# A decoder layer on one core: the Mamba work of four batches as one pipeline instead of two

## The chip, the cores and the metric

The kernel runs on one core of a Trainium2 chip. The metric is the time of one execution on the device in microseconds (us). Before the change three runs took 3520.11, 3522.89 and 3524.64 us; the median, 3522.89 us, is what the prediction is measured against.

## What is computed

One decoder layer, everything in float32, for 4 batches of 1024 tokens with 256 channels each:

```python
out1 = mb(rmsnorm(x, norm1_w))          # a Mamba block: projection, 4-tap convolution, selective scan, projection
x1   = x + out1
out2 = mb(rmsnorm(x1, norm2_w))         # the same Mamba weights a second time
out2 = memory_attend(out2, proj_write_w, proj_read_w, decay)
x = layernorm(x + (x1 + out2))
x = layernorm(x + cross_attention(x, context))      # 16 heads over 64 context tokens
x = layernorm(x + mixture_of_experts(x))            # best 2 of 8 experts
```

The heart of the Mamba block is a recurrence over the tokens, for 512 channels and 16 states:

```python
h = h * exp(d_t * A) + (d_t * u_t) * B_t
y = sum over states of h * C_t
```

The second Mamba pass of a batch needs the first pass's result (x1), and the second half of a batch's tokens needs the state h that the first half ended with. Batches don't depend on each other before the experts.

## The kernel before, in words

**Items, chunks and slots.** A batch's 1024 tokens are two halves of 512. One *item* is one half of one batch in one of the two passes: with u the batch within a pair, m the pass and h the half, the eight items of a pair come in the order u, then h, then m (`item_at`). An item has 64 *chunks*: one state and one block of 128 channels each. A chunk is one scan instruction of 128x512 on VectorE (`scan`, L1614), which takes its factors from ScalarE (`decay`, L931), its other input from a PSUM bank that TensorE fills by transposes (`fill`, L1181), and whose result GpSimd multiplies by a row of C (`weigh_c`, L720) and TensorE adds up (`add_y`, L1200). The time in which the 64 scans of one item run is called a *slot* below.

**The order is written out by hand.** Every engine runs the same loop `for c in range(-2 * CHUNKS, RUN + TAIL)`, and `when(c)` says which items are at which stage at chunk c: item s is scanned; item p = s + 1 goes through its input stage (normalise, project, convolve, make the step sizes); item p2 = s + 2 has its squares summed; item k = s - 1 leaves (gate, output projection). A table of numbers (`IN`, `SILU`, `SLOPE`, `TURN`, `MO` and so on) says at which of the 64 chunks each piece stands. So in the middle of the pipeline the scans of one item, the input stage of the next and the output stage of the one before share each slot. Two slots' worth of loop ahead of the first scan hold only input stages, and a tail of up to 64 chunks after the last scan holds only an output stage.

**Two groups.** `for g0 in range(GROUPS)` runs this pipeline twice, for batches 0 and 1 and for batches 2 and 3, eight items each. After each pipeline come the memory and the cross attention of that pair's two batches, one after the other (the *body* of a batch). `o2_dram` holds the second pass's result of the pair until its batch's body loads it. The buffers of the bodies and those of the pipeline lie in the same SBUF arena; only `xin` (x, later x1, of the two batches) keeps its place through both. After the second group come the experts.

**Names and lines used below.** VectorE: `convolve` (L1562), `sum_halo` (L1446 to L1455: what the second half needs of the first half's last three tokens), `times_u` (L1603), the multiply by the gate (L1535), the additions of `leave` (L1545 in pass 0, L1550 in pass 1), the normalisation that ends a body (L1521), the memset that begins one (L1652). GpSimd: `add_bias` (L672, one instruction of 128x1024 at the start of each pass-0 item's slot) and `normalise` (L685). `normalise` of a group's first item waits until the x2 of the batch before has been stored. SyncE issues the transfers in one queue, in this order: rows of C from `c_dram` (L581, four slots of buffer, one row for four chunks), `keep_o2` (L563), and in the bodies the loads of o2 (L596), x (L599), the next pair's x (L604) and the store of x2 (`keep_x2`, L548).

## Time and profile before

| what | value |
|---|---|
| median of 3 runs | 3522.89 us (3520.11 to 3524.64) |
| the profiled execution, first to last instruction | 3546.8 us |
| TensorE matmul / VectorE / ScalarE / GpSimd busy | 79% / 67% / 54% / 50% |
| first pipeline, first scan to last scan | 89.24 to 1067.75 us |
| bodies of batches 0 and 1 | to 1357.09 us |
| second pipeline, first scan to last scan | 1416.99 to 2395.36 us |
| bodies of batches 2 and 3 | to 2681.70 us |
| experts and the end | to 3546.8 us |

Of the profiled execution no other time than its span is on record; it is 23.9 us (0.7%) longer than the median of the runs. The profile's page gives busy shares over the whole span, which mixes stages with different limits. The view of busy time by stretch cuts the span at chosen times; here the cuts are the starts of the slots and the ends of the bodies, which the timeline of VectorE shows.

### The profile page before, as it was taken

How to read it: one execution, taken by the hardware profiler on the slowest of the kernel's cores; microseconds unless marked ns; L12 is line 12 of the kernel's file. 1: busy time of each engine (PE TensorE's matmuls, PEld its weight loads, DVE VectorE, ACT ScalarE, POOL GpSimd, SP SyncE). 2: the span in 40 equal slices, each digit the busy share in tenths (PEclk: the TensorE clock that was granted, in tenths of full speed). 3: DMA queues.
4: the chain of work that ended last, by engine and by line, in shares of the span. 5: the costliest groups of instructions: out<-in, count | busy, mean ns of one | idle time of the engine just before them, and what ended most of it. 6: DMA issues, size and time to landing. Idle time of an engine off the chain costs nothing.

```text
span 3546.8 us, 46325 instructions
## 1 busy us (share of the span) xinstructions
PE 2817.5 (79%) x15402; PEld 2084.2 (59%) x15403; DVE 2358.7 (67%) x3266; ACT 1928.5 (54%) x3239; POOL 1775.1 (50%) x1888
## 2 busy tenths in 40 slices
PE   3888788788887995788788788887996898999910
PEld 1666566666675653666566666675656665766600
DVE  3888988988882444888988988882444332333347
ACT  4877877887781324877887887771331111111100
POOL 1777767777781001777767777781100123222261
PEclk8998999999999896998999999999995799999955
DMA  3110111111111000011111111111102023122131
GB/s 107 31 36 32 34 36 34 34 36 41 40 44 55 28 9 25 31 37 32 35 34 34 34 37 39 40 46 54 36 1 86 33 79 132 49 77 78 50 96 55
DMA packets 101822, 163.32 MB, mean 46 GB/s; under 512 B 16610, under 2 KB 55778, under 8 KB 101634
## 3 DMA queue, kind: packets, MB, share of 16 engines
q1 hardware_dynamic: 80242, 109.94, 9.8%
q0 software_dynamic: 18064, 49.21, 4.1%
q8 instruction: 106, 1.74, 0.2%
q10 hardware_dynamic: 3328, 1.76, 0.2%
q14 instruction: 82, 0.67, 0.1%
HBM read 127.01 MB, written 24.38 MB: 43 GB/s over the span
## 4 chain that ended last, share of the span: by engine, by line
PE 42%; DVE 23%; ACT 13%; issue 11%; DMA 9%; POOL 1%; SPq 0%; another core or an unknown queue 0%; POOLq 0%; DVEq 0%; ACTq 0%
PE psD L1083 14%; DVE arena L1614 9%; PE psD L1181 6%; PE psA L1200 5%; ACT arena L931 4%; DMA write_w_sb<-x_dram,read_w_sb 4%; DMA write_w_sb<-write_w_sb 3%; ACT arena L921 3%; PE psD L1412 3%; DMA read_w_sb<-arena 2%; PE psD L1283 2%; PE psA L1083 2%; PE psA L1258 2%; PE psA L1190 2%; PE psD L1304 2%
## 5 line engine op out<-in xcount | busy, mean ns | idle before, releaser
L720 POOL TENSOR_TENSOR arena<-arena 128x512 f32<-128x512 f32 x1024 | 1154.2, 1154 | 17.8 <-DVE arena L1614 7.4
L1181 PE MATMUL psD<-ident,arena 128*128 128x128 f32 x4096 | 686.7, 293 | 344.4 <-DVE arena L1614 318.3
L1181 PEld LDWEIGHTS psD<-ident,arena 128*128 128x128 f32 x4096 | 482.3, 148 | 605.2 <-DVE arena L1614 375.8
L931 ACT ACTIVATE arena<-arena,negA 128x512 f32<-128x512 f32 x1024 | 719.2, 711 | 26.4 <-DVE arena L1614 25.7
L1614 DVE TENSOR_TENSOR_SCAN arena<-arena,carry,psD 128x512 f32<-128x512 f32 x512 | 641.9, 1269 | 83.3 <-PE psA L1200 75.2
L1614 DVE TENSOR_TENSOR_SCAN arena<-arena,psD 128x512 f32<-128x512 f32 x512 | 612.9, 1208 | 93.4 <-PE psA L1200 75.6
L1200 PE MATMUL psA<-ident,arena 128*128 128x128 f32 x4096 | 645.1, 283 | 0.0
L921 ACT ACTIVATE arena<-arena,bc 128x512 f32<-128x512 f32 x768 | 546.0, 711 | 118.3 <-PE psD L1181 117.6
L1200 PEld LDWEIGHTS psA<-ident,arena 128*128 128x128 f32 x4096 | 510.1, 148 | 2.1 <-issue 2.1
L704 POOL TENSOR_SCALAR arena<-arena,bc 128x512 f32<-128x512 f32 x256 | 180.8, 707 | 460.7 <-PE psD L1181 390.7
L1083 PE MATMUL psD<-arena 128*128 128x512 f32 (+4 forms) x776 | 336.1, 568 | 45.9 <-POOL strip L664 31.1
L1040 ACT ACTIVATE in_w_sb<-in_w_sb 128x512 f32<-128x512 f32 x140 | 88.1, 629 | 468.0 <-DVE in_w_sb L1812 468.0
L1412 PE MATMUL psD<-arena 128*128 128x256 f32 x1120 | 258.4, 384 | 2.9 <-DVE arena L1818 2.9
L823 ACT ACTIVATE arena<-psA 128x512 f32<-128x512 f32 x160 | 91.4, 597 | 300.5 <-PE psA L1258 117.2
L1083 PE MATMUL psD<-arena,in_w_sb 128*128 128x512 f32 x512 | 243.0, 598 | 6.5 <-DVE halo L1573 4.8
L1083 PEld LDWEIGHTS psD<-arena 128*128 128x128 f32 (+1 forms) x776 | 142.5, 194 | 153.0 <-issue 143.3
L1412 PEld LDWEIGHTS psD<-arena 128*128 128x128 f32 x1120 | 210.3, 193 | 31.4 <-DVE arena L1818 4.8
L1812 DVE TENSOR_TENSOR in_w_sb<-psD,arena 128x512 f32<-128x512 f32 x140 | 96.8, 691 | 166.0 <-PE psD L1083 166.0
L1823 DVE TENSOR_TENSOR arena<-psD,arena 128x256 f32 x70 | 29.7, 424 | 233.6 <-PE psD L1412 233.6
L1562 DVE SCALAR_TENSOR_TENSOR arena<-psD,conv_w_sb,arena 128x511 f32<-128x511 f32 (+2 forms) x192 | 140.1, 730 | 51.9 <-ACT arena L877 51.3
L742 POOL TENSOR_TENSOR arena<-arena 128x2048 f32<-128x2048 f32 x4 | 18.1, 4514 | 310.0 <-DMA arena<-in_x 310.0
L777 POOL DMA_INDIRECT write_w_sb<-x_dram,read_w_sb x70 | 69.6, 995 | 141.6 <-DMA read_w_sb<-arena 134.1
(230 smaller groups left out, 3840.8 us busy)
## 6 DMA issues: line engine op xcount, KB each, us to landing
arena<-c_dram SPq DMA_DIRECT2D x256, 256.0 KB, 3.1
arena<-in_W POOLq DMA_DIRECT2D x16, 1024.0 KB, 7.4
write_w_sb<-write_w_sb SPq DMA_DIRECT2D x72, 128.0 KB, 2.0
ys_dram<-arena POOLq DMA_DIRECT2D x70, 128.0 KB, 2.0
arena<-in_x SPq DMA_DIRECT2D x8, 1024.0 KB, 7.2
o_dram<-arena SPq DMA_DIRECT2D x32, 128.0 KB, 1.7
arena<-o_dram SPq DMA_DIRECT2D x4, 1024.0 KB, 5.4
x_dram<-arena SPq DMA_DIRECT2D x4, 1024.0 KB, 9.5
```

The lines of the kernel that those rows point to most:

```text
L704: pool.tensor_scalar(g[:, v % 2, JS, :], uT[:, i % 2, JS, :], bc[:, i % 2, JS, n:n + 1], 1.0, ALU.mult, ALU.mult).then_inc(b_by_pool, 1)
L720: pool.tensor_tensor(h_ring[:, c % H_SLOTS, :], h_ring[:, c % H_SLOTS, :], c_rows[:, v % C_SLOTS, :], ALU.mult).then_inc(c_weighed, 1)
L823: act.activation(dst, psA[:, bank, 0:width], func, **kw).then_inc(act_drained, 1)
L921: act.activation(g[:, v % 2, j, :], uT[:, i % 2, j, :], ACT.Copy, scale=bc[:, i % 2, j, n:n + 1])\
L931: act.activation(da_ring[:, c % DA_SLOTS, :], dt[:, i % 2, f, :], ACT.Exp, scale=negA[:, f, n:n + 1]).then_inc(da_ready, 1)
L1083: mm = pe.matmul(out_ap, lhs, rhs, start=i == 0, stop=i == len(pairs) - 1)
L1181: mm = pe.transpose(psD[:, c % FILL_BANKS, j * P:(j + 1) * P], g[:, (c // KI) % 2, j, c % KI * P:(c % KI + 1) * P], ident[:, :])
L1200: mm = pe.matmul(psA[:, f, j * P:(j + 1) * P], h_ring[:, c % H_SLOTS, j * P:(j + 1) * P], ident[:, :], is_transpose=True, start=False, sto ...
L1412: mm = pe.matmul(psD[:, 2, 0:D], hidT[:, k, :], w2_sb[:, r, k, :], start=k == 0, stop=k == KH - 1)
L1562: last = dve.scalar_tensor_tensor(xm[:, f, cols:], bank[:, 0:HALF - cols], conv_w_sb[:, f, tap:tap + 1], xm[:, f, cols:], op0=ALU.mult, op ...
L1614: dve.tensor_tensor_scan(h_ring[:, c % H_SLOTS, :], da_ring[:, c % DA_SLOTS, :], psD[:, c % FILL_BANKS, :], 0.0 if h == 0 else carry[:, u, ...
L1812: dve.tensor_tensor(hid[:, n * BANK:(n + 1) * BANK], psD[:, n, :], b1_sb[:, r, n * BANK:(n + 1) * BANK], ALU.add).then_inc(hid_ready, 1)
```

## The change

GROUPS goes, ITEMS becomes 16, and one pipeline runs through all four batches; the four bodies follow it in one loop. `item_at` now gives the pair too: items 0 to 7 are batches 0 and 1 as before, items 8 to 15 are batches 2 and 3. The waits count in one run of semaphore values. `xin` has room for two batches still, so three transfers are new, all in SyncE's queue among the rows of C: `keep_x1` stores each pass-0 item's half of x1 (8 stores of 128x4x256), and `next_x` loads x of batches 2 and 3 over batches 0 and 1 once those are normalised for the last time (slots 5 and 6), and x1 of batches 0 and 1 back (slots 13 and 14). The bodies of batches 2 and 3 load their x1 from `x1_dram` where the next pair's x was loaded before. `normalise` waits for no stored x2 any more.

The diff with the changes of indentation left out, cut to what the text speaks of:

```diff
-        o2_dram = nc.dram_tensor("o2_dram", (2, TT, P, D), F32, kind="Internal").ap()
+        o2_dram = nc.dram_tensor("o2_dram", (B, TT, P, D), F32, kind="Internal").ap()
+        x1_dram = nc.dram_tensor("x1_dram", (B, TT, P, D), F32, kind="Internal").ap()
...
-        ITEMS = 8
-        GROUPS = B // 2
+        ITEMS = 16
...
         def item_at(p):
-            q = p // 2
-            return p % 2, q, q // 2, q % 2
+            return p % 2, p // 8, p // 4 % 2, p // 2 % 2
+
+        def turn_of(p):
+
+            return p // 4 * 2 + p % 2
...
+            def keep_x1(i):
+                u, g0, m, h = item_at(i)
+                sp.wait_ge(bg_by_dve, taken("mo", i, JT - 1))
+                sp.dma_start(x1_dram[g0 * 2 + u, h * JT:(h + 1) * JT].rearrange("t p d -> p t d"),
+                             xin[:, u, h * JT:(h + 1) * JT, :]).then_inc(x1_stored[u], 16)
+
+            def next_x(i):
+                u, g0, m, h = item_at(i)
+                sp.wait_ge(normed, JT * (i + 1))
+                sp.wait_ge(x1_stored[u], 32 * (g0 + 1))
+                if g0 == 0:
+                    sp.dma_start(xin[:, u, :, :], x[2 + u].rearrange("(t p) d -> p t d", p=P)).then_inc(x_loaded[u], 16)
+                else:
+                    sp.dma_start(xin[:, u, :, :], x1_dram[u].rearrange("t p d -> p t d")).then_inc(x1_loaded[u], 16)
...
+                if n == 3 and i >= 2 and item_at(i - 2)[2] == 0:
+                    keep_x1(i - 2)
+                if n == 5 and i + 1 < ITEMS and item_at(i + 1)[2:] == (1, 1):
+                    next_x(i + 1)
...
-                for u in range(2):
-                    b = g0 * 2 + u
-                    if u == 0:
+            for b in range(B):
+                u = b % 2
+                if b == 0:
                         for r in range(2):
-                            sp.wait_ge(o2_stored[r], 16 * (g0 + 1) * ITEMS)
+                        sp.wait_ge(o2_stored[r], 16 * ITEMS)
...
                     if b + 2 < B:
-                        sp.dma_start(xin[:, u, :, :], x[b + 2].rearrange("(t p) d -> p t d", p=P)).then_inc(x_loaded[u], 16)
+                    sp.dma_start(xin[:, u, :, :], x1_dram[b + 2].rearrange("t p d -> p t d")).then_inc(x1_loaded[u], 16)
...
                 def normalise(i):
-                    u, q, m, h = item_at(i - i0)
-                    if i == i0:
-                        pool.wait_ge(x2_stored, g0 * 32 + 16)
-                    else:
+                u, g0, m, h = item_at(i)
+                if i > 0:
                         pool.wait_ge(bg_full, filled("xnT", i - 1, KD - 1))
...
-                    if s is not None and s < 4 and r == XB:
-                        add_bias(i0 + s)
+                if s is not None and item_at(s)[2] == 0 and r == XB:
+                    add_bias(s)
...
+                pool.wait_ge(x1_loaded[u], 16 * (b // 2 + 1))
```

How the order moves, at three places. First VectorE from the end of the slot of item 6 into that of item 7 (L1614 is the scan). Before, item 7 is the group's last:

```order
L1614 SCALAR_TENSOR_TENSOR arena<-arena,carry,psD 128x512 x3
L1550 TENSOR_TENSOR arena<-psD,out_b_sb 128x256
L1614 SCALAR_TENSOR_TENSOR arena<-arena,carry,psD 128x512 x50
L1535 TENSOR_TENSOR arena<-psD,arena 128x512
L1614 SCALAR_TENSOR_TENSOR arena<-arena,carry,psD 128x512 x3
```

and now (the scan is L1622, the convolution L1570, the halo L1580 and L1581):

```order
L1622 SCALAR_TENSOR_TENSOR arena<-arena,carry,psD 128x512 x3
L1558 TENSOR_TENSOR arena<-psD,out_b_sb 128x256
L1622 SCALAR_TENSOR_TENSOR arena<-arena,carry,psD 128x512 x11
L1570 SCALAR_TENSOR_TENSOR arena<-psD,conv_w_sb,arena 128x511
L1622 SCALAR_TENSOR_TENSOR arena<-arena,carry,psD 128x512
L1570 SCALAR_TENSOR_TENSOR arena<-psD,conv_w_sb,arena 128x510
L1622 SCALAR_TENSOR_TENSOR arena<-arena,carry,psD 128x512
L1570 SCALAR_TENSOR_TENSOR arena<-psD,conv_w_sb,arena 128x509
L1580 TENSOR_TENSOR arena<-arena,halo_sum 128x3
```

The input stage of item 8 now stands among the scans of item 7, where 50 scans stood in a row.

Second, VectorE at the end of the body of batch 1. Before, the second group's first input stage follows the normalisation:

```order
L1502 BN_STATS stats<-arena 128x6 x4
L1509 BN_AGGR aggr<-stats 128x2 x8
L1511 RECIPROCAL rs<-rt 128x8
L1521 TENSOR_SCALAR arena<-arena,aggr,rs 128x256 x8
L1562 SCALAR_TENSOR_TENSOR arena<-psD,conv_w_sb,arena 128x511
```

and now (normalisation L1531, memset L1660, the memory's products L1665):

```order
L1512 BN_STATS stats<-arena 128x6 x4
L1519 BN_AGGR aggr<-stats 128x2 x8
L1521 RECIPROCAL rs<-rt 128x8
L1531 TENSOR_SCALAR arena<-arena,aggr,rs 128x256 x8
L1660 MEMSET arena 128x2
L1665 TENSOR_TENSOR arena<-psD,strip 128x512 x2
```

The body of batch 2 follows that of batch 1 directly.

Third, SyncE's queue in slot 5, now (L601 rows of C, L572 `keep_x1`, L580 `next_x`, L562 the store of C of the next item, L567 `keep_o2`):

```order
L601 DMA arena<-c_dram 128x512 [waits c_weighed] x2
L572 DMA x_dram<-arena 128x4x256 [waits bg_by_dve]
L601 DMA arena<-c_dram 128x512 [waits c_weighed] x2
L580 DMA arena<-in_x 128x8x256 [waits x1_stored0,normed]
L601 DMA arena<-c_dram 128x512 [waits c_weighed] x3
L562 DMA c_dram<-arena 16x512 [waits bg_by_act]
```

Of these, L572 and L580 are new; the rows of C behind them stand as they did.

## Rows read from the trace of the kernel before

**Rows 1.** The profile's page: its span, and busy time, share and instructions of each engine.
```profile
span 3546.8 us, 46325 instructions
...
PE 2817.5 (79%) x15402; PEld 2084.2 (59%) x15403; DVE 2358.7 (67%) x3266; ACT 1928.5 (54%) x3239; POOL 1775.1 (50%) x1888
```

**Rows 2.** Timeline of VectorE at the edges: start, length, operation, count, idle before.
```profile
1066.47 1.28 DVE L1614 TENSOR_TENSOR_SCAN arena<-arena,carry,psD 128x512 f32<-128x512 f32 x1 [1.31 <-PE psA L1200]
...
1354.41 2.67 DVE L1521 TENSOR_SCALAR arena<-arena,aggr,rs 128x256 f32<-128x256 f32 x8
...
1416.99 2.33 DVE L1614 TENSOR_TENSOR_SCAN arena<-arena,psD 128x512 f32<-128x512 f32 x2 [5.93 <-ACT arena L931]
```

**Rows 3.** By stretch: length, busy PE, PEld, DVE, ACT, POOL (instructions), clock, DMA, GB/s.
```profile
89.24:207.13 117.89, 93.89 (x589) 71.19 (x588) 104.61 (x109) 98.00 (x163) 90.78 (x100) 0.94 0.10 32
207.13:338.89 131.76, 110.06 (x669) 87.35 (x668) 113.19 (x122) 102.48 (x171) 96.58 (x106) 0.91 0.11 33
338.89:468.75 129.86, 104.74 (x669) 81.33 (x668) 115.73 (x122) 102.27 (x171) 93.38 (x90) 0.96 0.10 34
468.75:595.74 126.99, 105.80 (x669) 81.74 (x668) 111.67 (x116) 101.89 (x171) 93.41 (x90) 0.95 0.12 34
595.74:721.02 125.28, 104.66 (x669) 82.01 (x668) 109.24 (x117) 101.86 (x171) 93.74 (x104) 0.96 0.12 35
721.02:846.03 125.01, 101.97 (x669) 78.93 (x668) 110.97 (x122) 101.95 (x171) 94.08 (x105) 0.99 0.13 39
846.03:972.16 126.13, 103.41 (x669) 80.03 (x668) 113.30 (x122) 100.32 (x161) 91.07 (x89) 0.97 0.13 39
972.16:1067.75 95.59, 84.71 (x600) 69.65 (x599) 83.02 (x72) 74.63 (x118) 80.09 (x81) 0.98 0.14 45
1067.75:1227.29 159.54, 134.39 (x597) 90.87 (x595) 57.87 (x136) 45.80 (x80) 11.31 (x4) 0.91 0.09 30
1227.29:1357.09 129.80, 115.34 (x480) 74.67 (x480) 53.63 (x127) 36.18 (x70) 10.24 (x3) 0.91 0.08 25
1357.09:1416.99 59.90, 28.62 (x66) 13.41 (x67) 25.03 (x44) 31.94 (x56) 10.64 (x12) 0.64 0.11 36
1416.99:1534.90 117.91, 93.91 (x589) 71.23 (x588) 104.63 (x108) 98.01 (x163) 90.79 (x100) 0.94 0.09 32
...
2299.84:2395.36 95.52, 84.73 (x600) 69.69 (x599) 83.01 (x72) 74.62 (x118) 80.16 (x81) 0.98 0.15 45
2395.36:2555.05 159.69, 134.67 (x597) 91.06 (x595) 57.87 (x135) 45.80 (x80) 11.31 (x4) 0.91 0.09 30
2555.05:2681.70 126.65, 112.71 (x480) 73.11 (x480) 53.50 (x126) 33.26 (x60) 10.22 (x3) 0.93 0.08 25
```

**Rows 4.** The same view of L1450 alone: length, busy VectorE (instructions), clock, DMA, GB/s.
```profile
207.13:338.89 131.76, 2.40 (x2) 0.91 0.11 33
...
721.02:846.03 125.01, 0.23 (x2) 0.99 0.13 39
```

**Rows 5.** The same view of L1603 alone, slot 4 and the stretch before slot 8.
```profile
595.74:721.02 125.28, 4.54 (x4) 0.96 0.12 35
...
1357.09:1416.99 59.90, 2.56 (x4) 0.64 0.11 36
```

**Rows 6.** The page's group of GpSimd's product: busy, mean ns, idle before, releaser.
```profile
L720 POOL TENSOR_TENSOR arena<-arena 128x512 f32<-128x512 f32 x1024 | 1154.2, 1154 | 17.8 <-DVE arena L1614 7.4
```

**Rows 7.** Transfers by line: out<-in, queue, count, KB each, us from issue to landing.
```profile
arena<-c_dram SPq DMA_DIRECT2D x256, 256.0 KB, 3.1
...
arena<-in_x SPq DMA_DIRECT2D x8, 1024.0 KB, 7.2
...
x_dram<-arena SPq DMA_DIRECT2D x4, 1024.0 KB, 9.5
...
arena<-x_dram SPq DMA_DIRECT2D x3, 1024.0 KB, 5.6
ys_dram<-arena SPq DMA_DIRECT2D x4, 512.0 KB, 5.8
```

More of the change, by code:

```diff
@@ L291, in decoder_layer @@
         x_loaded = [sem("x_loaded0"), sem("x_loaded1")]
+        x1_stored = [sem("x1_stored0"), sem("x1_stored1")]
+        x1_loaded = [sem("x1_loaded0"), sem("x1_loaded1")]
         o2_again = sem("o2_again")
@@ new lines, in add_bias, with normalise @@
+            def add_bias(i):
+                u, g0, m, h = item_at(i)
+                rows = xin[:, u, h * JT:(h + 1) * JT, :]
+                pool.tensor_tensor(rows, rows, out_b_sb[:, :].unsqueeze(1).broadcast_to([P, JT, D]), ALU.add)\
+                    .then_inc(xb_ready, 1)
+            def normalise(i):
+                u, g0, m, h = item_at(i)
+                if i > 0:
+                    pool.wait_ge(bg_full, filled("xnT", i - 1, KD - 1))
+                if i >= 3:
+                    pool.wait_ge(bg_full, filled("mo", i - 3, JT - 1))
+                pool.wait_ge(inverse, 2 * (i + 1))
+                for j in range(JT):
+                    pool.tensor_scalar(xn[:, j, :], xin[:, u, h * JT + j, :],
+                                       inv_rms[:, 1, j:j + 1], 1.0, ALU.mult, ALU.mult).then_inc(normed, 1)
@@ new lines, in _ @@
+            pool.wait_ge(w_loaded, LOADED)
+            for c in range(-2 * CHUNKS, RUN + TAIL):
+                r, k, s, p, p2 = when(c)
+                if (c + 6) % KI == 0 and 0 <= (c + 6) // KI < ITEMS * NS:
+                    spread_b((c + 6) // KI)
+                if 0 <= c - WEIGH_AFTER < RUN:
+                    weigh_c(c - WEIGH_AFTER)
+                if s is not None and item_at(s)[2] == 0 and r == XB:
+                    add_bias(s)
+                if p is not None and r == NORM:
+                    normalise(p)
+                if p is not None and r in CUBIC:
+                    soften(p, CUBIC.index(r))
@@ new lines, in times_u, with scan @@
+            def times_u(i, f):
+                dve.wait_ge(dt_ready, i * KI + f + 1)
+                dve.tensor_tensor(dtu[:, f, :], dt[:, i % 2, f, :], xm[:, f, :], ALU.mult).then_inc(dtu_ready, 1)
+            def scan(c):
+                q, n, f = chunk(c)
+                u, g0, m, h = item_at(q)
+                if f == 0 and h == 1:
+                    dve.wait_ge(carried, turn_of(q) * NS + n + 1)
+                if c >= H_SLOTS:
+                    dve.wait_ge(summed, c - H_SLOTS + 1)
+                dve.wait_ge(da_ready, c + 1)
+                dve.wait_ge(dbu_full, c + 1)
+                dve.tensor_tensor_scan(h_ring[:, c % H_SLOTS, :], da_ring[:, c % DA_SLOTS, :], psD[:, c % FILL_BANKS, :],
+                                       0.0 if h == 0 else carry[:, u, n, f:f + 1], ALU.mult, ALU.add)\
+                   .then_inc(scanned, 1)
@@ new lines, in _ @@
+            for c in range(-2 * CHUNKS, RUN + TAIL):
+                r, k, s, p, p2 = when(c)
+                if 0 <= c < RUN:
+                    scan(c)
+                if p is not None and r == 0 and item_at(p)[3] == 1:
+                    u, g0, m, h = item_at(p)
+                    dve.wait_ge(bg_by_dve, taken("in", p - 2, KI - 1))
+                    sum_halo(halo[:, 1 + u, :, :], halo_sum[:, 1 + u, :, :], 5 * (turn_of(p) + 1) + 4)
+                if k is not None and r - 2 in MO:
+                    leave(k, MO.index(r - 2))
+                if p is not None:
+                    for f in range(KI):
+                        for tap in range(TAPS - 1):
+                            if r == IN[f] + 4 - tap:
+                                convolve(p, f, tap)
+                    if r - 2 in Z:
+                        add_dt_b(p, Z.index(r - 2))
+                if k is not None and r - 1 in TURN:
+                    gate_y(k, TURN.index(r - 1))
+                if p is not None:
+                    for f in range(KI):
+                        if r == SMALL[f]:
+                            find_small(p, f)
+                        if r == SERIES[f]:
+                            expand(p, f)
+                        if r == REPLACE[f]:
+                            replace(p, f)
+                        if r == FINISH[f]:
+                            finish_dt(p, f)
+                        if r == TIMES[f]:
+                            times_u(p, f)
```

1232 lines of the change are left out of this document (573 added, 659 removed).

## The prediction

> **What bounds the kernel now.** I began with the page: VectorE is busy 67% of a span of 3546.8 us [rows 1], so no engine bounds the whole, and the reader should look for stages. The timeline of VectorE gives their edges [rows 2]: the first pipeline's last scan ends at 1066.47 + 1.28 = 1067.75, the body of batch 1 ends at 1354.41 + 2.67 = 1357.08, and the second pipeline's first scan starts at 1416.99. Then I cut the span at these edges and at the start of each slot and read busy time by stretch [rows 3]. There are three things to see. In slots 1 to 6 VectorE is busy for 109 to 116 of 125 to 132 us: it bounds the pipeline. Slot 7, which has no input stage beside it, takes only 95.59. And between 1357.09 and 1416.99 no engine is busy for more than 31.94 of 59.90 us: one input stage runs there alone, each engine waiting for the one before it. The second pair repeats the first almost exactly: slot 8 takes 117.91 where slot 0 takes 117.89, slot 15 takes 95.52 where slot 7 takes 95.59, batch 2's body 159.69 where batch 0's takes 159.54. So durations carry over from one place to its twin.
>
> **The change, part by part.** I write gains as plus.
>
> *The stretch before slot 8* goes: the body of batch 1 is followed by that of batch 2, not by an input stage. **+59.90** [rows 3]. The work in it doesn't vanish; it becomes the input stage beside slot 7, which is costed next.
>
> *Slot 7* now has the input stage of item 8 among its scans. Its nearest twin is slot 3 with 126.99: scans with a carried state, a next item that is a first half, an item that leaves. Slot 3 has one thing more, `add_bias`. What that costs comes from the pairs that differ by little else: slot 1 less slot 5 is 131.76 - 125.01 = 6.75, slot 2 less slot 6 is 129.86 - 126.13 = 3.73. Part of it is visible in VectorE's halo products, which take 2.40 us beside `add_bias` and 0.23 without [rows 4]; slots 3 and 7 have no such products, so the smaller figure is the bound. Slot 7 comes to between 126.99 - 3.73 = 123.3 and 127.0; I take 125.5, a little above the middle, since slot 6 (126.13) has the same scans. Against 95.5 that is **-30.0** (-27.8 to -31.5).
>
> The moved work costs more than it did alone, and that is already in these figures. `times_u`, which reads two operands from SBUF, takes 4.54 us for four beside GpSimd's products in slot 4, and 2.56 for four in the stretch where there are none [rows 5]: 0.50 us more each. The Trainium skill (SBUF — State Buffer, "Who interferes with whom") says that a VectorE instruction with two SBUF inputs and a GpSimd instruction that reads SBUF exclude each other, and the one that starts later blocks until the first has ended. By it each of them could wait for a whole product; I give that a place among the rivals, priced from rows.
>
> *Slot 8* now has the output stage of item 7, which slot 0 lacks. Its nearest twin without `add_bias` is slot 4 with 125.28; with `add_bias` and halo products as well it is slot 1 with 131.76. Slot 8 has `add_bias` but no halo products, so I add a little under 3.73 to slot 4 and take 128.5: **-10.6** against 117.91 (-7.4 to -13.9).
>
> *Slot 6* gets the four squares of item 8 on ScalarE. Slot 5 has them and takes 125.01, less than slot 6 without; ScalarE is busy 101.95 in slot 5 and 100.32 in slot 6. VectorE hides them: **0**, at most -1.6, their ScalarE time. If ScalarE became the bound they would cost that. Slots 0 to 5 and 9 to 15 hold the same compute instructions as before: 0.
>
> *The bodies.* A pair's first body, measured from the last scan, holds the output stage of the last item, the last stores of o2 and its way back through memory, with nothing beside them: 159.54 and 159.69. The following body takes 129.80 and 126.65 [rows 3]. Now only batch 0 is a first body, and batch 2 follows batch 1 as batch 1 follows batch 0. Batch 2 saves 159.69 less 128.2 (the mean of the two): **+31.5** (+29.9 to +33.0). Batch 2 now has x1 to wait for in GpSimd's addition; that load is issued when batch 0's x1 has been added, more than a whole body earlier, and such loads of 1 MB land in 5.6 to 7.2 us [rows 7], so over 120 us of body cover it. Without that cover it would hold the addition, and through it VectorE's use of `base`, by those 7 us. What is late next in the body is what was late in batch 1's.
>
> *The new transfers.* Eight stores of 512 KB and four loads of 1 MB now stand among the rows of C in SyncE's queue. A row of C serves four chunks, a sixteenth of a slot: 125 / 16 = 7.8 us. With four buffers it is issued about three rows, 23.4 us, before its use, and lands in 3.1 [rows 7], which leaves 20.3 spare. A transfer of 512 KB took 5.8 us, one of 1 MB 7.2, the slowest kind 9.5 [rows 7]. Even wholly ahead of a row these leave over 10 us. GpSimd's product, which uses the rows, idled 17.8 us over 1024 instructions, most of what is named on the scan [rows 6]. The waits in the queue should be over when SyncE comes to them: SyncE reaches `keep_x1` when all but four products of item i - 1 are done, at about chunk 0 of slot i, and it waits for the last addition of item i - 2, which stands at chunk 61 of slot i - 1; `next_x` comes two rows, eight chunks, later and waits for GpSimd's `normalise` of chunk 1. Behind both only rows of C are queued, and GpSimd's products wait for those. **0**, with a loss as a rival below.
>
> **The sum.** 59.9 - 30.0 - 10.6 + 31.5 = 50.8 us of the profiled 3546.8, which gives 3496.0, or 1.43%. The profiled execution is 23.9 us longer than the median of the runs; I carry the share over: 3522.9 x (1 - 0.0143) = **3472 us**. With the ends of the terms the gain is 59.9 + 33.0 - 27.8 - 7.4 = 57.7 at best and 59.9 + 29.9 - 31.5 - 13.9 - 1.6 = 42.8 at worst: 3466 to 3480.
>
> **The rivals.**
> *Whole products block the moved instructions.* Twelve moved instructions of VectorE in slot 7 read two SBUF operands (four each of L1587, L1599 and L1603; the predicated copies are left aside). If each waited for one whole product of 1.154 us [rows 6] instead of the 0.50 us above, slot 7 would take 12 x 0.65 = 7.8 us more: 3480. This is the rule of the Trainium skill's page at its hardest. For it: the halo products at 1.2 us each beside `add_bias` [rows 4]. Against it: in slot 4 the same instructions run beside the same products at 0.50 [rows 5].
> *Batch 2's body stays a first body.* If one of its loads (o2, x, x1) comes late because the queue holds it, batch 2 keeps 159.7 and the gain is 50.8 - 31.5 = 19.3: 3504. Against it: batches 1 and 3 load through the same queue with the same waits and take 126.65 and 129.80.
> *The seam doesn't close*, that is, the change doesn't do what it says: x of batches 2 and 3 is loaded into buffers that the first pair holds until slots 5 and 6, and the squares of item 8 want it in slot 6. If they found it late, the scans would stop by up to the 59.9 us that the change removes, slot 7 would stay short, and the gain would be 31.5 - 10.6 = 20.9: 3502. Against it: the load starts early in slot 5, a slot lasts 125 us and the load 7.2.
> *Slower: GpSimd waits for rows of C.* This has its place in the shared queue. If the spare time were none, each new transfer would hold the pipeline by its own length: 8 x 5.8 + 4 x 7.2 = 75.2 us, more than the gain, and the time would be 3522.9 + 24.2 = 3547. It decides once a transfer holds the queue for more than the 20.3 us of spare, and outweighs the gain from 4.2 us of standstill for each of the twelve (50.8 / 12). For it: all of them are in one queue with the rows. Against it: the spare time is twice the slowest transfer.
>
> **How the numbers follow.** The forecast gets 80%, for every term has a twin in the trace; blocked products 6%, batch 2's body 6%, the open seam 3%, the queue 5%. The range must leave out no more than 2 in 10: forecast and blocked products together hold 86%, and their bounds are 3466 to 3480. I widen that to 3462 to 3488, by the runs' own scatter (from 2.8 us below their median to 1.8 above) and for the carrying over of the share. No change within 0.2%, about 7 us, is what a measurement can't tell; every case but the queue lies below that, so 95% for faster, and of the queue's 5% one goes to no change, where its standstill just eats the gain, and four to slower.
>
> **What would show it.** In the changed kernel's profile, busy time by slot should give slot 7 at 123 to 127 us, slot 8 at 125 to 132, no pause between their scans, the other slots as before to 0.3 us, one body of about 159.6 and three of 126 to 130. The idle time before GpSimd's product should stay near 18 us. If slot 7 or 8 is over 135, or the slots with `next_x` or `keep_x1` (2 to 6 and 10 to 14) grow by several us, the prediction fails at the shared port or at the queue; if batch 2's body is near 160, at the loads.

## The result and the profile after

The changed kernel took a median of **3464.3 us** (3462.07 to 3470.55, four runs); the kernel before, run beside it, 3521.5 us. The ratio is 0.9844 with an interval of 0.9829 to 0.9860. The forecast was 3472 us with a range of 3462 to 3488: faster, as expected, and 7.7 us lower than the number.

The page of the changed kernel: span, busy time of the engines, GpSimd's product, and the transfers by line (out<-in, queue, count, KB each, us from issue to landing).

```profile
span 3460.3 us, 46348 instructions
...
PE 2783.7 (80%) x15402; PEld 2058.6 (59%) x15403; DVE 2362.6 (68%) x3266; ACT 1917.3 (55%) x3233; POOL 1785.6 (52%) x1888
...
L734 POOL TENSOR_TENSOR arena<-arena 128x512 f32<-128x512 f32 x1024 | 1157.8, 1156 | 14.1 <-DVE arena L1622 3.7
...
arena<-c_dram SPq DMA_DIRECT2D x256, 256.0 KB, 3.2
...
arena<-in_x SPq DMA_DIRECT2D x8, 1024.0 KB, 6.9
arena<-x_dram SPq DMA_DIRECT2D x7, 1024.0 KB, 5.6
x_dram<-arena SPq DMA_DIRECT2D x8, 512.0 KB, 4.5
```

The engines are busy for about as long as before [rows 1]: TensorE 34 us less, the others within 12 us. The change removes waiting, not work. The new transfers are in the last two rows (seven loads from `x_dram` instead of three, eight stores of 512 KB), and rows of C land in 3.2 us, before in 3.1 [rows 7].

Busy time by stretch, with the columns of [rows 3]: slots 7, 8 and 9, the four bodies in their order, and all that follows them.

```profile
975.06:1101.12 126.06, 103.33 (x669) 79.84 (x668) 111.70 (x116) 101.89 (x171) 90.81 (x89) 0.97 0.13 39
1101.12:1225.98 124.86, 103.32 (x669) 80.28 (x668) 109.13 (x116) 102.01 (x171) 96.71 (x105) 0.97 0.13 39
1225.98:1355.53 129.55, 106.09 (x669) 83.55 (x668) 113.09 (x121) 102.25 (x171) 96.38 (x106) 0.95 0.11 34
...
2081.83:2240.48 158.65, 133.60 (x597) 90.09 (x595) 58.02 (x135) 45.74 (x80) 11.31 (x4) 0.92 0.09 30
2240.48:2369.80 129.32, 116.74 (x496) 76.31 (x496) 53.53 (x127) 35.22 (x64) 10.23 (x3) 0.92 0.11 33
2369.80:2496.49 126.69, 114.49 (x496) 74.90 (x496) 53.52 (x127) 35.20 (x64) 10.23 (x3) 0.93 0.11 34
2496.49:2625.73 129.24, 115.06 (x480) 74.50 (x480) 53.54 (x127) 33.26 (x60) 10.24 (x3) 0.91 0.09 25
2625.73:3460.30 834.57, 632.93 (x2706) 451.70 (x2706) 355.97 (x837) 127.31 (x242) 243.15 (x312) 0.86 0.23 78
```

Slot 7 is a full slot now, and slot 8 follows it: item 7's last scan ends at 1099.81 and item 8's first starts at 1101.12, a gap of 1.31 us. One body is long and three are short. Up to the end of the last body the kernel needed 2681.70 us before and needs 2625.73 now, 55.97 less. In us, with gains as plus:

| part | forecast | measured |
|---|---|---|
| stretch between the pipelines | +59.9 | +59.9 |
| slot 7: 95.59 to 126.06 | -30.0 | -30.5 |
| slot 8: 117.91 to 124.86 | -10.6 | -7.0 |
| batch 2's body: 159.69 to 126.69 | +31.5 | +33.0 |
| slots 9 to 15 together | 0 | +4.6 |
| slots 0 to 6 together | 0 | -0.4 |
| first scan: 89.24 to 91.76 | 0 | -2.5 |
| other three bodies | 0 | -1.2 |
| sum | 50.8 | 55.9 |

What follows the last body took 834.57 us instead of 865.1 (3546.8 - 2681.70). That is 30.5 us more that the profiles seem to gain, in a part that the change doesn't touch; the first experiment below asks whether it is one.

### The profile page after: what moved, and what is told of

The parts are those of the page before. It is cut to its first block, busy times and chain, and to the rows that moved or that the text cites. A ratio compares the mean times of both kernels' runs of the same rounds, so it can differ in the third digit from the quotient of the medians.

```text
span 3460.3 us, 46348 instructions
## 1 busy us (share of the span) xinstructions
PE 2783.7 (80%) x15402; PEld 2058.6 (59%) x15403; DVE 2362.6 (68%) x3266; ACT 1917.3 (55%) x3233; POOL 1785.6 (52%) x1888
## 4 chain that ended last, share of the span: by engine, by line
PE 41%; DVE 23%; ACT 13%; issue 11%; DMA 10%; POOL 1%; SPq 1%; POOLq 0%; DVEq 0%; ACTq 0%
PE psD L1096 14%; DVE arena L1622 9%; PE psD L1192 5%; PE psA L1211 4%; ACT arena L944 4%; DMA write_w_sb<-x_dram,read_w_sb 4%; DMA write_w_sb<-write_w_sb 3%; ACT arena L934 3%; PE psD L1422 3%; DMA read_w_sb<-arena 2%; PE psA L1096 2%; PE psD L1293 2%; PE psA L1268 2%; PE psA L1201 2%; PE psD L1314 2%
## 5 line engine op out<-in xcount | busy, mean ns | idle before, releaser
L734 POOL TENSOR_TENSOR arena<-arena 128x512 f32<-128x512 f32 x1024 | 1157.8, 1156 | 14.1 <-DVE arena L1622 3.7
L1192 PE MATMUL psD<-ident,arena 128*128 128x128 f32 x4096 | 679.4, 291 | 356.4 <-DVE arena L1622 333.0
L1192 PEld LDWEIGHTS psD<-ident,arena 128*128 128x128 f32 x4096 | 477.0, 146 | 622.0 <-DVE arena L1622 390.4
L1622 DVE TENSOR_TENSOR_SCAN arena<-arena,carry,psD 128x512 f32<-128x512 f32 x512 | 643.2, 1269 | 79.8 <-PE psA L1211 68.1
L1622 DVE TENSOR_TENSOR_SCAN arena<-arena,psD 128x512 f32<-128x512 f32 x512 | 613.7, 1209 | 88.9 <-PE psA L1211 77.9
L1211 PE MATMUL psA<-ident,arena 128*128 128x128 f32 x4096 | 641.9, 282 | 0.0
L1211 PEld LDWEIGHTS psA<-ident,arena 128*128 128x128 f32 x4096 | 506.1, 147 | 1.1 <-issue 1.1
L1570 DVE SCALAR_TENSOR_TENSOR arena<-psD,conv_w_sb,arena 128x511 f32<-128x511 f32 (+2 forms) x192 | 139.9, 729 | 39.7 <-ACT arena L890 39.5
```

The source lines that it names most:

```text
L734: pool.tensor_tensor(h_ring[:, c % H_SLOTS, :], h_ring[:, c % H_SLOTS, :], c_rows[:, v % C_SLOTS, :], ALU.mult).then_inc(c_weighed, 1)
L1192: mm = pe.transpose(psD[:, c % FILL_BANKS, j * P:(j + 1) * P], g[:, (c // KI) % 2, j, c % KI * P:(c % KI + 1) * P], ident[:, :])
L1211: mm = pe.matmul(psA[:, f, j * P:(j + 1) * P], h_ring[:, c % H_SLOTS, j * P:(j + 1) * P], ident[:, :], is_transpose=True, start=False, sto ...
L1570: last = dve.scalar_tensor_tensor(xm[:, f, cols:], bank[:, 0:HALF - cols], conv_w_sb[:, f, tap:tap + 1], xm[:, f, cols:], op0=ALU.mult, op ...
L1622: dve.tensor_tensor_scan(h_ring[:, c % H_SLOTS, :], da_ring[:, c % DA_SLOTS, :], psD[:, c % FILL_BANKS, :], 0.0 if h == 0 else carry[:, u, ...
```

## The experiments

The questions were four: whether the profile of before was a fair base for the sum; how the gain divides between the closed seam and the joined bodies; whether the new transfers or a late load could hold anything; and what `add_bias`, which the prediction had only bounded, really costs. Each expectation sets the theory behind the prediction's terms (or the reading of the profile that had replaced one) against a rival for that question; I name both ahead of it in words. In the changed kernel `add_bias` is L688, `normalise` L699, GpSimd's product L734, and the halo sums are L1456, L1460 and L1465.

### The kernel before, once more

No edit. Either the long end of the profile of before was that one execution's, or the end is really shorter after the change.

> The kernel before, unchanged, for a second profile. In the first one its span stands 24 us over its own median, and the part behind the last body (experts and the end) takes 865.1 us against 834.6 in the profile of the changed kernel, which holds the same instructions. Theory 1, that stretch varies from run to run and the change has nothing to do with it: here it takes 830 to 845 us, the span comes within 5 us of the timed runs, and slots and bodies repeat to 0.3 us and 3 us. Theory 2, the change also shortens the experts: it takes about 865 us again.

It took 3519.28 us, its span is 3517.5. The last part of the span, in the profile of before and then in this one:

```profile
3400.00:3546.80 146.80, 0.00 (x0) 0.00 (x0) 103.61 (x276) 2.41 (x8) 57.16 (x55) 0.50 0.25 79
```

```profile
3400.00:3517.50 117.50, 0.00 (x0) 0.00 (x0) 103.47 (x276) 2.41 (x8) 57.59 (x51) 0.50 0.29 94
```

VectorE does the same work in both (103.6 and 103.5 us); the first only waits longer in it. After the last body this execution took 837.5 us, and the changed kernel 834.6. So the excess was that execution's own. Its slots also show how far two profiles of one kernel differ: slot 5 took 127.65 instead of 125.01, slot 9 129.50 instead of 131.77, slot 2 131.12 instead of 129.86. A difference of 2 to 3 us in one slot of one profile says nothing; sums over several slots say more. Its bodies end at 2679.98, so the gain up to there is 54.3 us by this profile and 56.0 by the other; the runs' is 3521.5 - 3464.3 = 57.2.

### Two empty slots at the seam

The bodies stay together, but items 7 and 8 are pulled apart by two slots' worth of loop, so that item 8's input stage and item 7's output stage stand alone again. The edit, cut to what does this (the rest of it moves the stores of o2 and of C at the seam and counts chunks without the hole):

```diff
+        SEAM, HOLE = 8, 2
...
+        def item_in(s):
+            return s if 0 <= s < SEAM else s - HOLE if SEAM + HOLE <= s < ITEMS + HOLE else None
...
-            items = [q if 0 <= q < ITEMS else None for q in (s - 1, s, s + 1, s + 2)]
+            items = [item_in(q) for q in (s - 1, s, s + 1, s + 2)]
```

The question is whether the two large terms of the sum are what they were taken for: a joined body and a closed seam, each with its own price, against one of them carrying nearly all.

> The changed kernel with two empty slots between items 7 and 8: the drain and the lone input stage stand between the two pairs again, but the four bodies stay together at the end. Theory 1, the seam gives its own part (about 60 us of lone input stage less some 37 us by which slots 7 and 8 grow) and the joined bodies give the rest (31 to 33 us): slot 7 falls to about 95 us, slot 8 to 118, a stretch of 70 to 85 us without scans (drain of 22 us and input stage of 60, the loads being early) stands between them, and the time is about 3464 + 75 - 31 - 7 = 3500 us, between 3490 and 3510. Theory 2, most of the gain is the joined bodies and the seam gives next to nothing: under 3475 us. Theory 3, the seam gives all: over 3515 us.

Measured: 3500.54 us (3497.96 to 3507.04), ratio 0.9955 (0.9940 to 0.9969). The pause between the scans and the slot after it:

```profile
1069.71:1144.45 74.74, 41.84 (x151) 24.98 (x150) 29.42 (x52) 41.67 (x76) 11.76 (x13) 0.77 0.07 22
1144.45:1261.93 117.48, 93.02 (x589) 70.68 (x588) 105.14 (x108) 97.94 (x163) 90.48 (x100) 0.94 0.10 32
```

Slot 7 is back at 95.44 (its scans end at 1069.71) and slot 8 at 117.5. Both parts stand as priced. The joined body brings 33.0 us, of which the pause takes back 74.74 - 59.90 = 14.8, since the output stage of item 7 now stands in it: 18.2, and the runs show 3519.8 - 3500.5 = 19.3 (the interval of the ratio spans 11 to 21). Closing this seam brings 74.74 less what slots 7 and 8 grow by (126.06 - 95.44 = 30.6, and 124.86 - 117.48 = 7.4): 36.7, and the runs show 3500.5 - 3464.3 = 36.2 (two rounds of runs, each with its own run of the kernel before; by their ratios it is some 39).

### Half the buffers for rows of C

```diff
-        DA_SLOTS, H_SLOTS, C_SLOTS = 6, 8, 4
+        DA_SLOTS, H_SLOTS, C_SLOTS = 6, 8, 2
```

The prediction put the new transfers at nothing because four buffers leave a row 20.3 us to spare. With two, a row is issued about one row ahead of its use. Either the transfers now hold GpSimd, as the slower rival said of a queue with no spare time, or something else than spare time protects it.

> The changed kernel with two buffers for rows of C instead of four. A row is then issued one row (7.8 us) ahead of its use and lands in 3.2, which leaves 4.6 us spare instead of 20. Theory 1, the new transfers cost nothing because of the spare time: now the loads of 1 MB (6.9 us) no longer fit and the stores of 512 KB (4.5 us) just do, so slots 5, 6, 13 and 14 grow by 2 to 5 us each, slots 2 to 4 and 10 to 12 by 0 to 2, slots 1, 7 and 9 by under 1, and the time by 8 to 30 us to 3472 to 3494. Theory 2, the queue has nothing to do with it, rows pass between the packets of the large transfers: no slot with a transfer grows by over 1 us more than slots 1 and 9 do.

Measured: 3463.97 us, ratio 0.9845 (0.9828 to 0.9861): as the change itself. GpSimd's product and the rows of C on its page:

```profile
L734 POOL TENSOR_TENSOR arena<-arena 128x512 f32<-128x512 f32 x1024 | 1158.9, 1158 | 14.1 <-DVE arena L1622 3.7
...
arena<-c_dram SPq DMA_DIRECT2D x256, 256.0 KB, 3.1
```

The product idles for the same 14.1 us. From landing to first use a row has a median of 5.1 us with two buffers (the least is 0.76) and 20.5 with four (the least 9.5). In the trace the row of C that follows a large transfer is issued 6.6 us or more after it. Nine of the twelve transfers have landed by then, the stores in 4.5 us; three loads of 1 MB still need 0.1 to 0.9 us, and the rows behind them land in 3.1 to 3.4 us all the same. So the distance between issues protects the rows here, and the spare time wasn't needed. Whether spare time would do without that distance no run shows. Slots 5 and 13, which hold a load, took 126.38 and 127.59 us instead of 124.90 and 125.12, no more than two profiles of one kernel differ.

### A late load in batch 2's body

```diff
+                if b == 2:
+                    sp.wait_ge(ln_done, b * 2 * TT)
                 sp.dma_start(o2, o2_dram[b].rearrange("t p d -> p t d")).then_inc(o2_again, 16)
```

Batch 2's o2 is loaded only when the body of batch 1 has ended. The rival "batch 2's body stays a first body" hung on a late load; the question is how much of a first body's extra 30 us a late load makes.

> The changed kernel with one more wait: SyncE loads o2 of batch 2 only when batch 1's body has ended. Theory 1, a following body is short because its o2 is there and turned before the body ahead ends: batch 2's body grows from 126.7 by the load (5.4 us) and the transposes behind it (3.5 to 8 us) to 136 to 141 us, and the time by 9 to 14 us to 3473 to 3479. Theory 2, something else holds the start of a body (VectorE's memset, the last normalisation): batch 2's body stays at 127 to 130 us, 3462 to 3467.

Measured: 3467.45 us, ratio 0.9862 (0.9845 to 0.9879). The body of batch 2:

```profile
2361.52:2494.97 133.45, 114.92 (x512) 76.02 (x512) 53.51 (x128) 37.50 (x68) 10.22 (x3) 0.93 0.12 40
```

Batch 2's body goes from 126.69 to 133.45, 6.8 us, less than was expected. In every other profile with the four bodies together it takes 126.7, so this is not scatter, though the runs' medians differ by only 3.2 us. The load itself lands in 5.4 us: where nothing covers it, it costs a little more than its own landing time. The rest of a first body's extra time is then not this load; the output stage of the last item and the stores of o2 are what else only it has, and no run took those apart. The rival's mechanism exists, but could not have cost 31.5 us by the load alone.

### `add_bias` in pieces, and whole at another place

Slot 8 has `add_bias` at chunk 1 like slot 1, but no halo products, and grew by 7.0 where 10.6 was forecast. It takes 124.86, and slot 4, which has neither, 125.35 in the same profile. So `add_bias` by itself seems free. Either it costs only where VectorE's halo products meet it, by its place, or by its length, one instruction of 2.37 us. Two kernels: four instructions of 128x256 at chunks 20 to 23, and the whole one at chunk 21, with no halo products near either.

```diff
-        XB, NORM = 1, 1
+        XB, NORM = [20, 21, 22, 23], 1
...
-                if s is not None and item_at(s)[2] == 0 and r == XB:
-                    add_bias(s)
+                if s is not None and item_at(s)[2] == 0 and r in XB:
+                    add_bias(s, XB.index(r))
```

> The changed kernel with add_bias cut into four instructions of 128x256, at chunks 20 to 23 of its slot instead of one of 128x1024 at chunk 1. Theory 1, add_bias costs where it stands beside the halo sums on VectorE (slots 1, 2, 9, 10) and hardly elsewhere: those four slots fall from 131.8, 129.8, 129.6 and 130.0 to 125 to 126.5, the slots 0, 3, 8 and 11 change by under 1 us, and the time falls by 13 to 20 us to about 3447. Theory 2, it costs its own length (2.4 us) wherever it stands in GpSimd's row: each of the eight slots stays within 1 us, no change in the time.

```diff
-        XB, NORM = 1, 1
+        XB, NORM = 21, 1
```

> The changed kernel with add_bias whole, but at chunk 21 instead of chunk 1. If the place alone matters (theory 1 of the split run), slots 1, 2, 9 and 10 fall to 125 to 127 us as in the split run, and the time is within 4 us of that run. If its length matters, because 2.4 us of GpSimd hold the products and the scans behind them wherever it stands, each of the eight slots takes 1 to 2.4 us more than in the split run: 8 to 19 us in all.

Measured: 3448.66 us in pieces, ratio 0.9797 (0.9778 to 0.9817), and 3448.64 whole, ratio 0.9804 (0.9787 to 0.9822). The place decides, not the length. Only the slots with both `add_bias` and halo products got shorter: slots 1, 2, 9 and 10 took 131.80, 129.81, 129.55 and 129.99 and take 125.04, 126.52, 127.66 and 126.51 with the whole one at chunk 21: 521.2 together, and 505.7. The other slots with `add_bias` hardly did: slots 0, 3, 8 and 11 went from 117.92, 127.00, 124.86 and 126.05 to 117.24, 126.04, 124.55 and 126.04, and the kernel before shows slot 3 at 127.00 in one profile and 126.03 in the other. By the medians both are 15.7 us below the changed kernel; the two were run in different rounds, and by the ratios it is 14 to 17.

Why it costs so much where the two meet is in the start of slot 1. VectorE of the changed kernel (start, length, operation, count, idle before and what ended it):

```profile
209.68 1.22 DVE L1622 TENSOR_TENSOR_SCAN arena<-arena,psD 128x512 f32<-128x512 f32 x1 [1.37 <-PE psA L1211]
210.82 1.08 DVE L1456 TENSOR_TENSOR halo_sum<-halo,conv_w_sb 128x12 f32<-128x12 f32 x1
211.83 2.41 DVE L1460 TENSOR_TENSOR halo_tmp<-halo,conv_w_sb 128x8 f32<-128x8 f32 x2
...
215.05 2.32 DVE L1622 TENSOR_TENSOR_SCAN arena<-arena,psD 128x512 f32<-128x512 f32 x2
218.32 1.22 DVE L1622 TENSOR_TENSOR_SCAN arena<-arena,psD 128x512 f32<-128x512 f32 x1 [0.95 <-PE psA L1211]
220.03 1.22 DVE L1622 TENSOR_TENSOR_SCAN arena<-arena,psD 128x512 f32<-128x512 f32 x1 [0.49 <-PE psA L1211]
```

GpSimd and TensorE of the same kernel there (L1192 and L1211 are the transposes into and out of the scans):

```profile
211.84 2.37 POOL L688 TENSOR_TENSOR arena<-arena,out_b_sb 128x1024 f32<-128x1024 f32 x1
214.18 1.85 POOL L699 TENSOR_SCALAR arena<-arena,inv_rms 128x256 f32<-128x256 f32 x4
```

```profile
212.51 0.60 PE L1211 MATMUL psA<-ident,arena 128*128 128x128 f32 x4
216.31 1.11 PE L1192 MATMUL psD<-ident,arena 128*128 128x128 f32 x4 [3.20 <-DVE arena L1622]
217.22 1.06 PE L1211 MATMUL psA<-ident,arena 128*128 128x128 f32 x4
```

And VectorE and GpSimd with `add_bias` at chunk 21:

```profile
208.31 1.07 DVE L1456 TENSOR_TENSOR halo_sum<-halo,conv_w_sb 128x12 f32<-128x12 f32 x1
209.31 0.23 DVE L1460 TENSOR_TENSOR halo_tmp<-halo,conv_w_sb 128x8 f32<-128x8 f32 x2
```

```profile
209.33 1.84 POOL L699 TENSOR_SCALAR arena<-arena,inv_rms 128x256 f32<-128x256 f32 x4
```

In the changed kernel the second halo product ends with `add_bias` (211.83 + 2.41 = 214.24, and 211.84 + 2.37 = 214.21); without it the two take 0.23. That holds VectorE for 2.2 us. But the ninth scan starts 226.81 - 209.68 = 17.1 us into the slot instead of 12.5, 4.6 later. The other 2.4 are TensorE's: its next transposes wait 3.20 us for the held scans, and when it goes on, four of them take 1.06 us instead of 0.60. The view of busy time by stretch, from the end of the hold to the seventh scan, and with `add_bias` late from the slot's start to the ninth:

```profile
215.05:223.44 8.39, 7.12 (x38) 7.12 (x39) 5.98 (x6) 5.07 (x9) 6.06 (x9) 0.59 0.09 33
```

```profile
207.17:219.68 12.51, 11.31 (x85) 9.40 (x84) 11.34 (x14) 11.69 (x21) 11.34 (x15) 1.00 0.13 44
```

The granted clock is 0.59 there, near the lower of the two levels (1.2 of 2.4 GHz), after full clock before the pause; with `add_bias` late it stays at 1.00. While it is low, TensorE sets the pace at 1.7 us a scan.

The hold and the clock can be told apart in the profile of the late o2, whose slot 1 is the same work. VectorE is held as long there and TensorE waits as long, but the granted clock stays at 1.00 (VectorE, TensorE, and the stretch from the slot's start to the ninth scan; line numbers there are higher by two):

```profile
207.52 2.41 DVE L1462 TENSOR_TENSOR halo_tmp<-halo,conv_w_sb 128x8 f32<-128x8 f32 x2
210.74 8.64 DVE L1624 TENSOR_TENSOR_SCAN arena<-arena,psD 128x512 f32<-128x512 f32 x7
```

```profile
212.01 0.66 PE L1194 MATMUL psD<-ident,arena 128*128 128x128 f32 x4 [3.21 <-DVE arena L1624]
```

```profile
205.37:220.21 14.84, 11.29 (x85) 9.40 (x84) 13.68 (x13) 11.68 (x21) 13.67 (x16) 1.00 0.11 37
```

So the hold alone moves the ninth scan from 12.5 to 14.84, 2.3 us, and the fallen clock adds another 2.3. Slot 9 of the profiles with the empty slots and with two buffers agrees: the clock doesn't fall there either, and the ninth scan starts after 14.84 and 14.83. By the slot's end the difference is 6.8 in the changed kernel and 3.4 with the late o2 (128.44 less 125.04). I did not follow the last 2.2 of the 6.8.

### The halo sums elsewhere

The opposite move: `add_bias` stays at chunk 1 and the halo sums go to chunk 5, where no `add_bias` is. The rivals were that this frees the same time as moving `add_bias`, or that the halo sums find something else to wait for.

```diff
-                if p is not None and r == 0 and item_at(p)[3] == 1:
+                if p is not None and r == 5 and item_at(p)[3] == 1:
```

> The changed kernel with VectorE's halo sums at chunk 5 instead of chunk 0 of their slot; add_bias stays at chunk 1. Theory 1, in slots 1, 2, 9 and 10 the halo sums are held by add_bias and the scans behind them wait: taking them away from it does what moving add_bias did, those slots fall to 125 to 127 us and the time to 3447 to 3454 us. Theory 2, it was GpSimd's row that cost (add_bias and normalise, 4.2 us together, ahead of its products), and the halo sums only show it: no slot changes by over 1 us, 3462 to 3467 us.

Measured: 3471.35 us, ratio 0.9865 (0.9848 to 0.9881): no gain, rather a loss, and neither number. VectorE in slot 2, and GpSimd there:

```profile
342.73 2.54 DVE L1456 TENSOR_TENSOR halo_sum<-halo,conv_w_sb 128x12 f32<-128x12 f32 x1
345.19 4.98 DVE L1460 TENSOR_TENSOR halo_tmp<-halo,conv_w_sb 128x8 f32<-128x8 f32 x2
```

```profile
340.96 4.24 POOL L734 TENSOR_TENSOR arena<-arena 128x512 f32<-128x512 f32 x4
...
345.83 4.24 POOL L734 TENSOR_TENSOR arena<-arena 128x512 f32<-128x512 f32 x4
```

Here four products stand in a row, and the tiny sums wait until the last of a row has ended: 342.73 + 2.54 against 340.96 + 4.24, 345.19 + 4.98 against 345.83 + 4.24. TensorE then stands for 7.83 us:

```profile
351.94 1.09 PE L1192 MATMUL psD<-ident,arena 128*128 128x128 f32 x4 [7.83 <-DVE arena L1622]
```

But slot 2, which takes 136.48 us instead of 129.81, is the only one of the eight where this happens. In the others a sum waits for the end of the one product that it meets, 1.13 us at most, and runs before the next. VectorE and GpSimd in slot 10, beside such a row:

```profile
1367.01 2.17 DVE L1460 TENSOR_TENSOR halo_tmp<-halo,conv_w_sb 128x8 f32<-128x8 f32 x2
```

```profile
1364.91 4.25 POOL L734 TENSOR_TENSOR arena<-arena 128x512 f32<-128x512 f32 x4
```

Slots 5, 6, 13 and 14, which had no `add_bias` to get away from, still grow by 1.1 to 3.7 us each, 10.9 together. At chunk 0 part of the sums stands in a wait of VectorE for TensorE (the last experiment shows it); here they stand among scans that follow each other.

With both moved (`add_bias` at chunk 21, halo sums at chunk 5):

> The changed kernel with add_bias at chunk 21 and the halo sums at chunk 5. If one conflict is behind both (theory 1), this gives what either move gives alone, within 5 us of 3448.6. If the two moves take away different costs, they add up: about 3433 us.

Measured: 3464.32 us, ratio 0.9843 (0.9826 to 0.9859). What the one move gives, the other takes back. Against the changed kernel slots 1, 2, 9 and 10 take 511.4 instead of 521.2 together. Slots 5, 6, 13 and 14, which have halo sums and no `add_bias`, went from 124.90, 126.52, 125.12 and 126.15 to 130.3, 129.0, 130.3 and 128.9.

The last pair kept `add_bias` at chunk 21 and put the halo sums at chunk 1 (`r == 1` in the line above), beside the same kernel with the sums at chunk 0. The sums at chunk 0 still meet one product (L1456 takes 1.07 us above), so they might have something left to gain.

> The changed kernel with add_bias at chunk 21 and the halo sums at chunk 1, where GpSimd runs normalise (four instructions with one tensor input, 1.84 us). In e_halo_late a halo sum that met GpSimd's products waited until the last product of their row had ended (2.5 and 4.2 us) and ran in 0.2 us beside an instruction with one tensor input. Theory 1, it is products and add_bias, with two tensor inputs, that hold a halo sum: the first one, 1.08 us at chunk 0 beside a product, falls to 0.15 to 0.3, eight slots fall by up to 1 us each, and the time is 3440 to 3447 us. Theory 2, any instruction of GpSimd that reads SBUF holds it: five sums wait for four pieces of normalise, 1.8 us each time, and the time rises to 3450 to 3460.

> The kernel of e_bias_late once more, on the chip of e_halo_next, so that the two can be compared: 3445 to 3453 us.

Measured: 3448.43 us (3445.03 to 3453.64) against 3449.79 (3444.63 to 3452.12), both with a ratio of 0.9796: no difference, a miss. The sums themselves did get faster. VectorE at the start of slot 1 with them at chunk 1:

```profile
208.92 1.22 DVE L1622 TENSOR_TENSOR_SCAN arena<-arena,psD 128x512 f32<-128x512 f32 x1 [1.37 <-PE psA L1211]
211.51 1.22 DVE L1622 TENSOR_TENSOR_SCAN arena<-arena,psD 128x512 f32<-128x512 f32 x1 [1.37 <-PE psA L1211]
212.65 0.29 DVE L1456 TENSOR_TENSOR halo_sum<-halo,conv_w_sb 128x12 f32<-128x12 f32 x1
```

At chunk 0 they stood in the 1.37 us that VectorE waits for TensorE before the second scan, and cost little there: the second scan started 210.21 - 207.17 = 3.04 us after the first with them, and 211.51 - 208.92 = 2.59 without. Now that wait shows as idle time, and the sums come after it.

## Why the prediction was right, and where its terms were off

**Right by its own steps.** Slot 7 was to be 123 to 127 us and is 126.06; no pause at the seam; one body of about 159.6 and three of 126 to 130, and they are 158.65, 129.32, 126.69 and 129.24. The two large terms were +59.9 for the stretch less 30.0 for slot 7, and +31.5 for batch 2's body; they measured 59.9, 30.5 and 33.0, and the kernel with the empty slots shows that they are two separate gains. Twins in the trace were the reason for these numbers, and they held. The total was closer to the edge than the terms: 3464.3 lies below the 3466 that the best ends of all terms gave, and is in the range because that was widened for the runs' scatter. That part was luck. Of the 7.7 us 1.4 are the base, since the kernel before came out at 3521.5 beside the changed one; slot 8 makes 3.6 and batch 2's body 1.5.

**Slot 8 was mis-sized**: "I add a little under 3.73 to slot 4", -10.6 where -7.0 was measured, just under the 125 to 132 that the text named. The 3.73 was the difference of slots with and without `add_bias` that all have halo products. The text saw that the halo products wait for `add_bias` [rows 4], and took the smaller difference as a bound, but still carried it to a slot without such products. There it is zero: the cost belongs to the meeting, as the moved `add_bias` shows. Slot 7's middle value was short by 0.5 us.

**Batch 2's body** was taken as the mean of batches 1 and 3 and came out at the lower of the two: 1.5 us. The other slots were to stay "as before to 0.3 us", which no profile could have shown: two of the kernel before differ by 2.6 in one slot. The first scan starts at 91.76 in this profile, at 89.94 with `add_bias` at chunk 21 and at 88.06 with the late o2, so its 2.5 are scatter. Slots 9 to 15 are another matter. They add up to 860.5 and 859.5 in the two profiles of before, and to 855.8, 856.8 and 855.8 in those of the change, of the change with two buffers and of the change with the late o2; with the empty slots, which open the seam again, it is 856.9. Half of the 4.6 is in slot 9, 131.77 and 129.55, where the clock after the hold made the difference: up to the ninth scan the granted clock was 0.80 over 17.13 us in before and 0.89 over 16.05 now. That varies from profile to profile: the second profile of before has 129.51 in slot 9. Whether some 3 us of the rest are real stays open, and I have no cause for them.

**The base.** The sum was carried over as a share because the profile was 23.9 us long. That execution's excess lay behind the last body, so the plain difference was the right reading: 3522.9 - 50.8 = 3472.1. The share made 0.4 us of difference only because the gain is small.

**The transfers** were put at nothing, and it is nothing: the product idles 14.1 us, less than the 17.8 of before, since the 3.7 us that it idled in slot 7 are gone. The reason given was spare time; halving the buffers shows that it wasn't needed. The price of the slower rival, eight stores of 5.8 us each, was high too; they land in 4.5.

**The rival of the shared port** was given 6% for the moved instructions, and as it was priced, at a whole product for each, it didn't come: the four `times_u` of slot 7 take 4.63 us, and 4.54 in slot 4 of before [rows 5]. But its mechanism is in these figures. The 0.50 us was read as a small loss of each; it is a mean of waits from nothing to the rest of a product. VectorE and then GpSimd in slot 7 (`times_u` is L1611, L1595 another of the moved instructions):

```profile
1057.96 1.44 DVE L1611 TENSOR_TENSOR arena<-arena 128x512 f32<-128x512 f32 x1
1060.52 0.66 DVE L1611 TENSOR_TENSOR arena<-arena 128x512 f32<-128x512 f32 x1
1065.02 1.05 DVE L1595 SCALAR_TENSOR_TENSOR arena<-arena 128x512 f32<-128x512 f32 x1
```

```profile
1056.28 2.58 POOL L734 TENSOR_TENSOR arena<-arena 128x512 f32<-128x512 f32 x2
1058.81 1.71 POOL L706 TENSOR_TENSOR arena<-arena 128x512 f32<-128x512 f32 x1
1060.49 1.64 POOL L734 TENSOR_TENSOR arena<-arena 128x512 f32<-128x512 f32 x1
1064.84 0.69 POOL L718 TENSOR_SCALAR arena<-arena,bc 128x512 f32<-128x512 f32 x1
```

The first ends 0.54 us after the product that it met (1059.40 against 1058.86), the third 0.54 after a tensor_scalar (1066.07 against 1065.53), and the second, which starts as one instruction of GpSimd gives way to the next, takes 0.66 and is not held; the product beside it takes 1.64 instead of about 1.07. The price carried over because the order of the two engines repeats from slot to slot. By the rule of the Trainium skill (SBUF — State Buffer, "Who interferes with whom") a VectorE instruction with two SBUF inputs contends with a GpSimd instruction that reads SBUF, and the later one blocks. These rows agree with that, and so do the halo products beside `add_bias`; what the halo sums add is in the last section.

## What to carry to other kernels

Joining two pipelines is worth the fill and drain between them less what the freed slots grow by, and both can be read from twins in the trace: here to 0.5 us for a slot whose twin had the same neighbours, and to 3.6 for one whose twin had not. The cost of an instruction that two kinds of slots share must be taken from a pair that differs in that instruction alone; if the loss arises where it meets another one, moving either is the test, and the other must be moved to a place that has been looked at for its own neighbours. A small hold on one engine should be priced with what it starves: here 2.2 us on VectorE stayed 2.3 where TensorE kept its clock, and became 4.6 where the clock fell. A mean over several instances (here 0.50 us each) should be taken apart before it is read as what each of them costs.

## What the runs showed of the hardware

- **A VectorE instruction with two SBUF inputs waits for the end of the GpSimd instruction that it meets, whether that is a tensor_tensor or a tensor_scalar.** Besides the rows of slot 7, the second halo sum at chunk 0 of the changed kernel takes 0.42 us in each of its eight slots and ends 0.01 us after a piece of `normalise`; ahead of the first scan, with nothing beside it, it takes 0.17. The section of the Trainium skill, which speaks of any GpSimd instruction that reads SBUF, agrees. Two halo products that started within 0.05 us of the start of such a piece were not held (0.23 us for both).
- **Once it was held for a whole row of GpSimd's.** In one of eight slots the two products of 128x8 took 4.98 us beside four back-to-back tensor_tensors of 4.24 us together, and did not get in between them; in another slot, beside the same row, they did (2.17 us). What decides between the two is open.
- **A pause of TensorE of 3.2 us was followed by a fall of the granted clock in 21 of 24 places, and by none in 3.** The 24 are slots 1, 2, 9 and 10 of the six profiles in which `add_bias` and the halo sums meet. In the changed kernel's slot 1 the clock was then 0.59 over 8.39 us; in the three, the ninth scan started 14.8 us into the slot instead of 15.7 to 17.1. In the kernel with the halo sums at chunk 5 a pause of 7.83 us left four transposes at 1.09 us.
- **A large transfer did not delay the small ones behind it in one queue**, where these were issued 6.6 us or more later: rows of C landed in 3.0 to 3.4 us behind transfers of 512 KB and 1 MB.
